# First attention: the zeros for the top-4 layer's slots are issued on ScalarE's queue instead of SyncE's

## The reference, cut to what matters

```python
x = x + 0.5 * _L0_ffn_ref(_layernorm(x))   # top-1 of 8 experts
x = x + _L0_attn_ref(_layernorm(x))        # the first attention
x = x + 0.5 * _L0_ffn_ref(_layernorm(x))
x = x + 0.5 * _L1_ffn_ref(_layernorm(x))   # top-4 of 32 experts, and a shared one
x = x + _L1_attn_ref(_layernorm(x))
x = x + 0.5 * _L1_ffn_ref(_layernorm(x))
```

```python
scores = jnp.einsum('bqhrd,bkhd->bhrqk', q, k) * scale
scores = jnp.where(causal, scores, jnp.finfo(scores.dtype).min)
probs = jax.nn.softmax(scores, axis=-1)
y = jnp.einsum('bhrqk,bkhd->bqhrd', probs, v)
```

## Time and profile before

| | |
|---|---|
| median of three runs | 1868.67 us (1867.82 to 1871.08) |
| the profiled execution's own time | 1873.8 us |
| its span, first to last instruction | 1872.0 us |
| first attention, about 236 to 434 us of the span | 10% of it |
| zero pieces in it | 24 DMAs of 512 KB, 250.6 to 380.8 us |

### The profile page before, as it was taken

How to read it: one execution, slowest core, us unless ns; L and a number is a source line. 1 busy time by engine, 2 the same in 40 slices (tenths; PEclk the granted TensorE clock), 3 DMA queues, 4 the chain that set the end, 5 groups by cost and what they waited for, 6 DMA issues and landing times.

```text
span 1872.0 us, 34469 instructions
## 1 busy us (share of the span) xinstructions
PE 1221.8 (65%) x11513; PEld 902.4 (48%) x11545; DVE 1135.0 (61%) x2883; ACT 785.3 (42%) x1164; POOL 968.9 (52%) x1052
## 2 busy tenths in 40 slices
PE   2298577874594165979654578777874085979661
PEld 2297455653494024968522244444433035969420
DVE  6546756767357951424467699898987942325442
ACT  2153356661252022534311388887883022535210
POOL 0624234551623276636675377666651376646664
PEclk9998789995796577989967555555555587989886
DMA  9233134410231013645311000000000014536312
GB/s 348 65 96 95 36 123 149 147 54 2 93 90 43 13 49 109 197 132 185 124 48 42 13 2 2 2 1 2 1 2 1 23 48 139 188 131 192 96 49 78
DMA packets 100000, 150.44 MB, mean 80 GB/s; under 512 B 21409, under 2 KB 54817, under 8 KB 99105
## 3 DMA queue, kind: packets, MB, share of 16 engines
q1 hardware_dynamic: 58656, 75.30, 12.3%
q0 software_dynamic: 20480, 41.98, 7.5%
q10 hardware_dynamic: 20736, 31.47, 5.2%
HBM read 74.16 MB, written 74.45 MB: 79 GB/s over the span
## 4 chain that ended last, share of the span: by engine, by line
PE 33%; POOL 19%; DVE 18%; issue 14%; DMA 8%; SPq 4%; ACT 2%; DVEq 0%; ACTq 0%; another core or an unknown queue 0%; POOLq 0%
POOL slots_top L624 14%; POOL AREA L1086 5%; PE PS L845 4%; PE PS L906 4%; DMA slots_top<-XN,ROW 3%; PE PS L298 3%; SPq L1285 3%; DVE X L1107 3%; PE PS L300 3%; PE PS L299 3%; PE PS L1729 2%; PE PS L928 2%; DVE AREA L1895 2%; PE PS L1745 2%; PE PS L1717 2%
## 5 line engine op out<-in xcount | busy, mean ns | idle before, releaser
L624 POOL DMA_INDIRECT slots_top<-XN,ROW x320 | 317.3, 992 | 322.8 <-DVE ROW L578 183.6
L1086 POOL DMA_INDIRECT AREA<-results_top,ROW x320 | 305.2, 954 | 275.2 <-DMA results_top<-AREA 125.1
L998 DVE SCALAR_TENSOR_TENSOR AREA<-PS,AREA 128x512 f32<-128x512 f32 x96 | 66.4, 691 | 254.2 <-ACT AREA L975 251.6
L1690 POOL TENSOR_TENSOR AREA<-AREA 128x1024 f16<-128x1024 f32 x64 | 151.4, 2365 | 91.5 <-ACT AREA L1830 91.3
L906 PE MATMUL PS<-WGU,AREA 128*128 x768 | 187.0, 388 | 0.0
L1919 DVE TENSOR_REDUCE AREA<-PS 128x4 f32<-128x1024 f32 x128 | 156.1, 1219 | 30.4 <-PE PS L1717 29.6
L1823 ACT ACTIVATE AREA<-PS,AREA 128x1024 f32<-128x1024 f32 x128 | 142.6, 1114 | 53.1 <-PE PS L1729 52.9
L906 PEld LDWEIGHTS PS<-WGU,AREA 128*128 128x128 f32 x768 | 142.3, 195 | 16.5 <-ACT AREA L965 0.2
L1318 POOL TENSOR_TENSOR AREA<-AREA 128x1536 f16<-128x1536 f32 x32 | 92.9, 2902 | 102.7 <-ACT AREA L1533 102.7
L417 PE MATMUL PS<-IDF,XN 128*128 128x128 f32 x192 | 49.7, 417 | 134.6 <-DVE XN L407 134.6
L1830 ACT ACTIVATE AREA<-AREA 128x1024 f16<-128x1024 f32 x128 | 135.5, 1059 | 0.0
(11 more groups left out here) (260 smaller groups left out, 3584.9 us busy)
## 6 DMA issues: line engine op xcount, KB each, us to landing
AREA<-slots_top SPq DMA_DIRECT2D x96, 256.0 KB
results_top<-AREA ACTq DMA_DIRECT2D x96, 256.0 KB
slots_top<-ZERO SPq DMA_DIRECT2D x24, 512.0 KB, 3.1
AREA<-slots_top SPq DMA_DIRECT2D x48, 128.0 KB
results_top<-AREA ACTq DMA_DIRECT2D x48, 128.0 KB
AREA<-query_rows SPq DMA_DIRECT2D x48, 128.0 KB, 2.8
slots_top<-XN,ROW POOLq DMA_INDIRECT x320, 2.2
AREA<-results_top,ROW POOLq DMA_INDIRECT x320
```

The source lines that it names most:

```text
L624: nc.gpsimd.indirect_dma_start(out=L.xs[q], out_offset=bass.IndirectOffsetOnAxis(ap=ROW[:, n:n + 1], axis=0), in_=XN[:, t * D:(t + 1) * D] ...
L1086: nc.gpsimd.indirect_dma_start(out=slots[L.tag][u][:, c * D:(c + 1) * D], out_offset=None, in_=L.ys[g * GT // L.tiles], in_offset=bass.Ind ...
L1690: nc.gpsimd.tensor_tensor(PB1[1][:, g, :], PF1[:, g, :], PB1[0][:, g, :], ALU.subtract).then_inc(b_plo[1].sem, 1)
```

## The change

The call of zero_slots leaves the end of SyncE's slot and stands at the end of ScalarE's slot, behind exp(t) and p_hi(t). Pieces, addresses, sizes and the semaphore are the same. SyncE's issue of the two top-1 pieces at the start stays as it is.

```diff
-        def zero_slots(sp, L, piece):
+        def zero_slots(eng, L, piece):
...
-            sp.dma_start(xs[:, at:at + n, :], ZERO[:, :].unsqueeze(1).to_broadcast([P, n, GT * D])
+            eng.dma_start(xs[:, at:at + n, :], ZERO[:, :].unsqueeze(1).to_broadcast([P, n, GT * D])
                          ).then_inc(filled[L.tag].sem, 16)
...
                 if q_batch(t, 1) is not None:
                     q_write(q_batch(t, 1))
-                if 0 <= t < ZERO_PIECES["top4"]:
-                    zero_slots(sp, L1, t)
...
                 if exists(t):
                     exp(t)
                     p_hi(t)
+                if 0 <= t < ZERO_PIECES["top4"]:
+                    zero_slots(nc.scalar, L1, t)
```

## The result

The change makes the kernel slower by a little: 1871.53 us against 1868.1 us (medians of 19 runs each), a ratio of 1.002 with a 95% interval of 1.0011 to 1.0029. That is 2.1 to 5.4 us more, where 3.5 us less was forecast.

The account below looks back on a forecast made before the run. SyncE's queue was taken to bound the stretch, chiefly issuing the maxima's rows (30.1%). A 3.7 us relief, less 0.2 for transfers and 0 for ScalarE's issue, gave 3.5: 1868.7 - 3.5 = 1865.2 us, range 1858 to 1875.

Parts of the forecast that it names:

- Part 1: SyncE's queue: removing the twelve even zero pieces gains 2.5 to 4.8 us; the odd ones give 0.
- the middle of the estimate: SyncE's gain taken as 3.7 us, between 2.5 by the chain and 4.8 by the slacks.
- The slack: Time from max_copy's end to the even unit's rows on SyncE, 0.02 to 1.27 us; capped at 0.62 each, 4.8 us.
- Part 2: ScalarE's queue: each piece's issue, about 0.53 us, is covered by p_hi, so price 0; 0.7 per piece if uncovered.
- lock on the descriptor block: Descriptor generation shared by both issuing queues: the 0.58 us would return as a lock wait of SyncE's rows; taken as 0.
- Part 3: Transfers: even pieces run earlier, beside the odd unit's rows; loss 12 x 0.02 = 0.2 us, odd pieces unpriced.
- The bound of 9.6: Largest loss from transfers: 12 x 0.8 us, if each delay of rows near a piece landed on the chain.
- 0.2 us at the median: Delay of rows near a piece: landing in 1.9 us behind one, 1.7 without; 0.8 at worst.
- the fourth, the collision: Even pieces collide with the odd unit's rows, which land late: +4.8 us, 1873.5; chance 0.12.
- The first rival: Earlier rows shorten TensorE's idle time; half the falls to its low clock go, 5 us more gain, 1860; chance 0.15.
- count of pairs with a fall: Pairs with TensorE's clock falling, units 2 to 24, now four; the prediction fails if it changes by two.
- the slower rivals: ScalarE's issue not covered by p_hi, 1873.6, chance 0.11; even pieces colliding with odd rows, 1873.5, chance 0.12.

Follow-up runs that it names:

- six_tiny: six_after with each zero piece on ScalarE's queue replaced by a 64-byte DMA at the same place; 2436.53 us.
- six_before: The kernel before with its phases replaced by top-1 layer and first attention six times, zero pieces on SyncE's queue; 2447.26 us.
- six_after: six_before with the zero pieces on ScalarE's queue, as in the changed kernel; 2471.98 us.
- six_none: six_before without any zero piece for the top-4 layer and without the final wait for them; 2429.12 us.
- six_before_b: six_before run once more, as base on the same chip for the split of even and odd pieces; 2448.0 us.
- set 2: Six attentions in one run: pieces on SyncE 2447.26 us, on ScalarE 2471.98, none 2429.12, tiny transfers on ScalarE 2436.53.
- set 4: Against six_before_b at 2448.0 us: even pieces alone on ScalarE 2472.81, odd alone 2467.59, both in odd slots on SyncE 2453.52.
- six_odd: six_before with only the odd pieces moved to ScalarE's queue; 2623.69 us on set 3's chip, 2467.59 us repeated in set 4.
- set 3: Six attentions, another chip: TensorE waits filled, pieces on SyncE 2636.39 us, on ScalarE 2657.47; unfilled, even piece a slot later 2649.62, only odd moved 2623.69.

## Why the prediction was wrong

**Part 1, the relief: size near, way wrong.** Without any pieces an attention gains 3.0 us where 3.7 was the middle of the estimate. With the issues on ScalarE and hardly any transfer (six_tiny) it is 1.8. But it doesn't come as 0.6 us less of SyncE's turn at each even piece: pairs at the high clock take 10.58 us without pieces and 10.64 with them. In the trace after, the even unit's rows start within 0.1 us of the end of max_copy for nine of the twelve units, where the prediction counted three so close: SyncE had the time back and spent it waiting. The slack was against one of several loops of nearly one length; that the others, over the landing, TensorE and ScalarE, closed the gap is the likely reading. In the profiles the gain shows as fewer pairs with a fall, 11 instead of 21. So the nearness of the size is luck.

**Part 2, ScalarE's queue: right.** The issue starts 0.01 to 0.02 us behind p_hi's start, takes 0.38 us instead of the estimated 0.53 and is covered. That two issuers hold each other up isn't seen: SyncE's rows take 590 ns at the median with and without. A median hides single long issues, so the sum counts too: from the first exp to that of unit 24 the issues of the rows take 62.0 us per attention in six_before, 62.1 in six_after, and 60.4 in both six_none and six_tiny. The reads' issues take 22.3 in six_none and 23.7 in six_tiny, so a small part may be there. The Trainium skill's lock on the descriptor block ("Perfetto Trace Analysis", DMA Instruction — HWDGE), by which the issue on SyncE would have been longer, doesn't show in the rows' numbers.

**Part 3, the transfers: this step failed.** It had the facts: the even piece comes 2.5 us earlier, beside the odd unit's rows, which are the more sensitive, and rows near a piece land 0.2 to 0.8 us later. Then it set the price at 12 x 0.02 = 0.2 us, since what one group of rows loses the other gains. The netting nearly held for the landings (even rows 0.3 us earlier, odd ones 0.45 later), but the two groups aren't worth the same. The even unit's rows, issued behind a piece before, had time: by_key followed 3.3 us after their last issue in six_before_b. The odd unit's by_key starts as its rows land, 1.9 us after. The delay of those is 0.56 us on average. The transfers of all 24 pieces cost 5.9 us per attention, not 0.2. The bound of 9.6 that was written down held it, the value taken did not. How much of the 5.9 goes through the odd rows isn't settled: the even pieces alone make the full loss with that delay, but the odd pieces alone cost nearly as much without it, and Part 3 had priced those at nothing. Its "0.2 us at the median" also rested on two groups of four rows.

**The rival that came out** is the fourth, the collision, given 12%, for the even pieces; its sign, odd rows landing later than 2.5 us, was badly chosen. The trace after shows it (3.6 at worst), and so did the one before (3.5); what moved is the median of the odd rows, from 1.9 to 2.5. The first rival was right that the clock moves with TensorE's waits, with the wrong sign. Its count of pairs with a fall, on which the whole prediction was to hang, is four in both traces and tells nothing: one attention is too small a sample. That the time lies inside the range of 1858 to 1875 is no merit of the sum, for that part of the range was there for the slower rivals.

**The profile against the runs.** A single profile of after has a shorter attention than before, and the runs say +3.4 us in the median. A forecast of 3.5 us rested on sums from one execution whose repetitions scatter by more than that.

The rule in the Trainium skill that a second issuing queue only saves the sequencer's issue time ("DMA: Bandwidth & Descriptors", Issuing engines are not separate DMA queues) is borne out as far as nothing but SyncE's issue time was saved here. It says that the transfers interleave; what that costs a small transfer it doesn't say. Here the queue's order had also fixed beside which small transfers a large one ran.

## What to carry to other kernels

The place of a large transfer in a queue also fixes beside which small ones it runs. Before it is moved to another queue, list which small transfer will be in flight at its new moment and who waits for that one. Price such a delay by the slack of the waiter, each group for itself, never by netting one group against another. And for effects of 0.2% repeat the stage several times in one program: six attentions told the parts of the loss apart in five or six runs each, where twelve runs with one attention left either half at anything from 0.02 to 0.28%.

## What was not expected of the hardware

- Pairs of units took 10.5 to 10.6 us on average in all four kernels of set 2, or 12.8 to 13.5 with a fall of TensorE's clock; what changed was mainly the number of falls, 11, 19, 21 or 27 of 66. Of the longer time between the places of the pieces, TensorE's busy time at the lower clock is 9 of 31 us in set 2 and 12 of 19 in set 4 (sums over six windows), so the clock is a part of the cause and not the whole.
- A DMA issue on ScalarE's queue is free beneath an activation at 0.38 us, and takes 1.31 us when the pieces before it are still being moved.
- With 16 matmuls per unit in TensorE's waits the time at the low clock was 4 us per attention, where it was 17.8 in six_odd, unfilled, on the same chip. No gain in time shows: the filled kernel was not faster than six_odd (set 3).
